# Expert results stored by token through an indirect write, and read back with plain loads, in a one-core decoder layer

## What is computed

```python
def ffn(x, gate_w, gate_b, w1, b1, w2, b2):           # E = 8 experts, K = 2, F = 1024
    gate_probs = softmax(x @ gate_w + gate_b)
    weights, selected = top_k(gate_probs, K)
    weights = weights / sum(weights)
    comb = zeros((n, E)).at[arange(n)[:, None], selected].set(weights)
    h = gelu(einsum('nd,edf->enf', x, w1) + b1[:, None, :])
    expert_out = einsum('enf,efd->end', h, w2) + b2[:, None, :]
    return einsum('ne,end->nd', comb, expert_out)
...
x = layernorm(x + ffn(x, ...))
```

## Time and profile before

| | us |
|---|---|
| median of 3 runs | 587.74 (585.92 to 588.46) |
| time of the profiled execution | 587.59 |
| its span, first to last instruction | 585.5 |
| PE busy (share of the span) | 541.9 (93%) |
| DVE busy | 359.4 (61%) |
| ACT busy | 316.2 (54%) |
| POOL busy | 170.4 (29%) |
| bytes moved by DMA | 58.77 MB, 100 GB/s on average |

### The profile page before, as it was taken

How to read it: one execution, slowest core, us unless ns; L and a number is a source line. 1 busy time by engine, 2 the same in 40 slices (tenths; PEclk the granted TensorE clock), 3 DMA queues, 4 the chain that set the end, 5 groups by cost and what they waited for, 6 DMA issues and landing times. The chain is left out here.

```text
span 585.5 us, 12747 instructions
## 1 busy us (share of the span) xinstructions
PE 541.9 (93%) x3908; PEld 470.8 (80%) x3908; DVE 359.4 (61%) x1136; ACT 316.2 (54%) x862; POOL 170.4 (29%) x280
## 2 busy tenths in 40 slices
PE   5999999999999999999999999989889999999920
PEld 3989899898998989899887666655479999999920
DVE  3365655657556565655567767787585656666645
ACT  4564554645545455454546787756553545545613
POOL 3511312113131221300445758442630000000353
PEclk9999999999999999999999999999799999999975
DMA  7850310405004050182000000020212535444224
GB/s 252 299 198 20 148 69 18 179 18 191 24 28 169 18 197 0 59 346 114 2 2 1 1 3 4 3 74 24 95 46 60 218 137 189 180 181 180 64 81 125
DMA packets 18420, 58.77 MB, mean 100 GB/s; under 512 B 3184, under 2 KB 7536, under 8 KB 13776
## 3 DMA queue, kind: packets, MB, share of 16 engines
q1 hardware_dynamic: 13920, 37.74, 17.9%
q10 hardware_dynamic: 1872, 12.85, 5.8%
q0 software_dynamic: 2592, 7.74, 3.9%
HBM read 35.83 MB, written 22.41 MB: 99 GB/s over the span
## 5 line engine op out<-in xcount | busy, mean ns | idle before, releaser
L1337 ACT ACTIVATE hT<-bank,b 128x128 f32<-128x128 f32 x152 | 53.7, 367 | 60.1 <-PE bank L954 56.5
L954 PE MATMUL bank<-xgT,w 128*128 128x128 f32 x608 | 71.2, 275 | 0.8 <-DVE xgT L1644 0.8
L954 PEld LDWEIGHTS bank<-xgT,w 128*128 128x128 f32 x608 | 69.6, 192 | 1.1 <-issue 1.0
L1089 ACT ACTIVATE Pr<-Sm,nmax 128x128 f32<-128x128 f32 x64 | 25.8, 403 | 70.7 <-DVE nmax L1398 70.6
L616 PE MATMUL bank<-xT_hi,wqk_hi 128*128 128x512 f32 x128 | 56.8, 444 | 7.1 <-DVE wqk_lo L1389 6.4
L1398 DVE CUSTOM_DVE_ANT_0 Sm<-bank,mask 128x128 f32<-128x128 f32 (+1 forms) x128 | 40.7, 355 | 30.2 <-PE bank L660 30.2
L1537 DVE TENSOR_REDUCE xnmax<-bank 128x2 f32<-128x512 f32 x64 | 43.5, 687 | 16.2 <-PE bank L818 15.6
L618 PE MATMUL bank<-xT_hi,wqk_lo 128*128 128x512 f32 x128 | 51.2, 400 | 0.0
L617 PE MATMUL bank<-xT_lo,wqk_hi 128*128 128x512 f32 x128 | 50.8, 397 | 0.0
L1199 ACT ACTIVATE xPT<-bank 128x512 f32<-128x512 f32 x64 | 37.7, 595 | 16.3 <-PE bank L839 16.1
L1420 DVE TENSOR_TENSOR z_lo<-bank,z_hi 128x256 fp32r<-128x256 f32 x64 | 27.1, 423 | 30.7 <-ACT z_hi L1082 30.5
(11 more groups left out here) (245 smaller groups left out, 1491.8 us busy)
## 6 DMA issues: line engine op xcount, KB each, us to landing
w<-in_w ACTq DMA_DIRECT2D x12, 1024.0 KB, 6.2
x_slots<-w SPq DMA_DIRECT2D x8, 1024.0 KB, 5.5
w_raw<-in_w_attn SPq DMA_DIRECT2D x31, 256.0 KB, 3.6
y_slots<-w SPq DMA_DIRECT2D x7, 1024.0 KB, 7.4
w<-in_w SPq DMA_DIRECT2D x4, 1024.0 KB, 7.9
y_slots<-ys POOLq DMA_DIRECT2D x19, 128.0 KB, 2.1
xg<-x_slots SPq DMA_DIRECT2D x18, 128.0 KB, 2.0
acc<-in_x SPq DMA_DIRECT2D x1, 1024.0 KB, 9.0
```

The lines of the kernel that those rows point to most:

```text
L954: last = mm(ps_h[f % 4][:, 0:P], w1[e % 2][:, c, f * P:(f + 1) * P], xgT[:, c, :], start=c == 0, stop=c == DC - 1)
L1337: A(hT[:, f, :], ps_h[f % 4][:, 0:P], ACT.Gelu_apprx_tanh, bias=b1[:, e, f:f + 1])\
```

## The change

- A row of `x_slots` grows from 256 to 258 numbers. The two at its end are the token's row number, 2 + 2\*token, and the lower of its two experts. `acc` gets the two columns in SBUF (`acc_rows`); an iota and one small DVE operation in each `slots(r)` fill them. `x_slots` is filled with zeros in 16 pieces of 128 x 1032 numbers, and `y_slots` with none.
- `y_slots` is replaced by a table `y_rows` of 2050 rows of 256: rows 2 + 2\*token and 3 + 2\*token are a token's results of its lower and its higher expert. Rows 0 and 1 take what unused slots give.
- Per tile, DVE computes `row_i` from the two numbers (`rows_of`), and copies the next tile's two numbers out of `xg` (`token`) right before the copy to `xgT`. POOL stores `ys` by an indirect DMA through `row_i`.
- The wait for the store of the tile before (`y_stored`) leaves `y_add` and now stands in `rows_of`, ahead of the copy to `xgT`. SP loads `xg` after the copy to `xgT` of the tile before (`xgt_ready`) and not after its transposes (`xgt_done`).
- One plain load from POOL brings all of `y_lo`; eight plain loads from SP bring `y_hi`.

The core of the diff:

```diff
+    W = D + 2
+    ZROWS = N // 2
+    ZFILLS = E * CAP // ZROWS
-        acc = sb(ctx, "acc", [P, TT, D])
+        acc_rows = sb(ctx, "acc", [P, TT, W])
+        acc = acc_rows[:, :, 0:D]
...
+        y_pairs = ys_d[2:2 * N + 2, :].rearrange("(t p k) d -> p t k d", p=P, k=2)
...
                 with sp.Fori(lo, hi) as i:
-                    sp.wait_ge(s["xgt_done"], i + 1)
+                    sp.wait_ge(s["xgt_ready"], i)
...
+            sp.wait_ge(s["y_stored"], lo * 16)
+            sp.nop(nofuse=True)
+            for t in range(TT):
+                sp.dma_start(y_hi[:, t, :], y_pairs[:, t, 1, :]).then_inc(s[f"yhi_in{t}"], 16)
...
                         g.indirect_dma_start(xs_d, bass.IndirectOffsetOnAxis(ap=slot_i[:, t, k:k + 1], axis=0),
-                                             acc[:, t, :], None).then_inc(s["xs_written"], 16)
+                                             acc_rows[:, t, :], None).then_inc(s["xs_written"], 16)
...
+            def store_rows():
+                g.indirect_dma_start(ys_d, bass.IndirectOffsetOnAxis(ap=row_i[:, 0:1], axis=0), ys[:, :], None)\
+                    .then_inc(s["y_stored"], 16)
...
-                    for t in range(TT):
-                        g.indirect_dma_start(y_lo[:, t, :], None, ys_d,
-                                             bass.IndirectOffsetOnAxis(ap=slot_i[:, t, 0:1], axis=0))\
-                            .then_inc(s["ylo_in"], 16)
+                    g.dma_start(y_lo[:, :, :], y_pairs[:, :, 0, :]).then_inc(s["ylo_in"], 16)
...
+            def rows_of(e, i, pair):
+                if not (isinstance(i, int) and i == 0):
+                    dve.wait_ge(s["y_stored"], i * 16)
+                v.scalar_tensor_tensor(out=row_i[:, :], in0=pair[:, 1:2], scalar=float(e), in1=pair[:, 0:1],
+                                       op0=ALU.is_lt, op1=ALU.add).then_inc(s["rows_ready"], 1)
+
-            def xgt_evac(count_done):
+            def xgt_evac(count_done, take=True):
                 dve.wait_ge(s["xgt_done"], count_done)
+                if take:
+                    v.tensor_copy(token[:, :], xg[:, D:W]).then_inc(s["token_ready"], 1)
...
             def y_add(e, i):
                 dve.wait_ge(s["y_done"], i + 2)
-                dve.wait_ge(s["y_stored"], i * 16 + 16)
...
                 with dve.Fori(lo, hi) as i:
                     h_splits(i)
+                    dve.wait_ge(s["token_ready"], i + 1)
+                    rows_of(e, i, token[:, :])
+                    dve.wait_ge(s["rows_ready"], i + 1)
                     xgt_evac(i + 3)
                     y_add(e, i)
```

More of the change, by code:

```diff
@@ L107, in build_decoder_layer @@
         w_lh = sb(ctx, "w_lh", [P, TT, 2])
+        token = sb(ctx, "token", [P, 2])
+        row_i = sb(ctx, "row_i", [P, 1], i32)
         tiles_i = sb(ctx, "tiles_i", [P, E], i32)
@@ L179, in build_decoder_layer @@
         hT_lo = sb(s3, "hT_lo", [P, FC, P], f32r)
-        xg = sb(s3, "xg", [P, D])
         xgT = sb(s3, "xgT", [P, DC, P])
-        xg_s = sb(s3, "xg_s", [P, EARLY, D])
+        xg_s = sb(s3, "xg_s", [P, EARLY, W])
         w2_hi1 = sb(s3, "w2_hi1", [P, FC, D], f32r)
+        xg = sb(s3, "xg", [P, W])
         ys = sb(s3, "ys", [P, D])
@@ L287, in _ @@
             half = N // 2
+            zero_rows = w1[0][:, :, :].rearrange("p c f -> p (c f)")[:, 0:ZROWS // P * W]
             for c in range(DC):
@@ L320, in next_parts @@
                 sp.dma_start(w_raw[:, 3, :], w_attn_d[bass.ds(p + 1, 1), :, 3, :]).then_inc(s["wo_in"], 16)
[L321 to L324, removed]
+                for k in range(2):
+                    sp.dma_start(xs_d[bass.ds((2 * p + k) * ZROWS, ZROWS), :].rearrange("(a b) d -> a (b d)", a=P),
+                                 zero_rows).then_inc(s["slots_zeroed"], 16)
                 sp.wait_ge(s["wqk_split"], 2 * p + 4)
@@ L331, in _ @@
             sp.dma_start(w_raw[:, 3, :], w_attn_d[PAIRS - 1, :, 3, :]).then_inc(s["wo_in"], 16)
[L332 to L336, removed]
+            for k in range(2 * (PAIRS - 2), ZFILLS):
+                sp.dma_start(xs_d[k * ZROWS:(k + 1) * ZROWS, :].rearrange("(a b) d -> a (b d)", a=P),
+                             zero_rows).then_inc(s["slots_zeroed"], 16)
+            sp.wait_ge(s["slots_zeroed"], 16 * ZFILLS)
             for e in range(2):
@@ L386, in _ @@
             pool.sem_inc(s["y_evac"], 1)
+            pool.sem_inc(s["token_ready"], 2)
             g.memset(ident[:, :], 0.0).then_inc(s["zeroed"], 1)
@@ L405, in _ @@
                    allow_small_or_imprecise_dtypes=True).then_inc(s["ident_ready"], 1)
+            g.iota(acc_rows[:, :, D], pattern=[[2 * P, TT]], base=2, channel_multiplier=2,
+                   allow_small_or_imprecise_dtypes=True).then_inc(s["ident_ready"], 1)
             g.iota(iota_slot[:, :], pattern=[[CAP, E]], base=0, channel_multiplier=0,
@@ L554, in _ @@
             for e in range(E):
-                skip = pool.value_load(first_i[0:1, e:e + 1], min_val=0, max_val=N // P - 1) if e < EARLY else 0
                 hi = pool.value_load(cum_i[0:1, e:e + 1], min_val=EARLY + 1, max_val=EARLY + 3 * E)
                 if e == E - 1:
-                    pool.wait_ge(s["y_stored"], lo * 16 + 16)
+                    pool.wait_ge(s["y_stored"], lo * 16)
                     pool.nop(nofuse=True)
-                    for t in range(TT):
-                        g.indirect_dma_start(y_lo[:, t, :], None, ys_d,
-                                             bass.IndirectOffsetOnAxis(ap=slot_i[:, t, 0:1], axis=0))\
-                            .then_inc(s["ylo_in"], 16)
+                    g.dma_start(y_lo[:, :, :], y_pairs[:, :, 0, :]).then_inc(s["ylo_in"], 16)
                 with pool.Fori(lo, hi) as i:
                     pool.wait_ge(s["y_evac"], i + 2)
-                    row = nc.s_assert_within((i - lo + skip) * P + e * CAP, e * CAP, (e + 1) * CAP - P,
-                                             skip_runtime_bounds_check_because="an expert has at most CAP tokens")
-                    g.dma_start(ys_d[bass.ds(row, P), :], ys[:, :]).then_inc(s["y_stored"], 16)
+                    pool.nop(nofuse=True)
+                    store_rows()
                 lo = hi
[L571 to L575, removed]
         def o_bank(p, t):
@@ L759, in _ @@
                 v_unit(0, t)
-            pe.wait_ge(s["ident_ready"], 7)
+            pe.wait_ge(s["ident_ready"], 8)
             pairs_loop(pe, attend)
@@ L1774, in _ @@
             gate_select(2)
-            xgt_evac(2)
+            xgt_evac(2, take=False)
             slots(2)
@@ L1784, in _ @@
                 if e == 0:
-                    xgt_evac(e + 3)
+                    rows_of(e, e, xg_s[:, e, D:W])
+                    xgt_evac(e + 3, take=False)
                     y_add(e, e)
@@ L1789, in _ @@
                     slot_weights()
+                    rows_of(e, e, xg_s[:, e, D:W])
+                    xgt_evac(e + 3)
                     y_add(e, e)
-                    xgt_evac(e + 3)
             lo = EARLY
@@ L1881 @@
     slots = g["L0_ffn_w1"].shape[0] * x.shape[0]
-    args.append(nc.dram_tensor("x_slots", (slots, x.shape[1]), mybir.dt.float32, kind="Internal").ap())
-    args.append(nc.dram_tensor("y_slots", (slots, x.shape[1]), mybir.dt.float32, kind="Internal").ap())
+    args.append(nc.dram_tensor("x_slots", (slots, x.shape[1] + 2), mybir.dt.float32, kind="Internal").ap())
+    args.append(nc.dram_tensor("y_rows", (2 * x.shape[0] + 2, x.shape[1]), mybir.dt.float32, kind="Internal").ap())
     out = nc.dram_tensor("out", (P, tiles, x.shape[1]), mybir.dt.float32, kind="ExternalOutput").ap()
```

14 lines of the change are left out of this document (6 added, 8 removed).

## The result

| | before | changed |
|---|---|---|
| median of the timed runs, us | 587.59 (4 runs) | 598.93 (4 runs, 598.19 to 600.85) |
| profiled execution, us | 587.59 | 600.85 |
| its span | 585.5 | 598.6 |

The changed kernel is slower, clear of the noise and by about 2%: 1.0201 times the time before, 95% interval 1.0169 to 1.0234. The forecast was 592.4 us, 584 to 600. So the direction and the range held, but the loss is 11.3 us in the medians where 4.8 were expected. The two profiles lie 13.1 us apart, and the balance goes by them.

The account below looks back on a forecast made before the run. PE was taken as busy nearly all the time until its last matmul at 560.03 us, then a 25.47 us chain follows. 587.59 + 11.6 (waits) - 6.8 (end) = 592.4 us; range 584 to 600.

Parts of the forecast that it names:

- Part 1: Expert tiles: the store wait ahead of the copy to `xgT` makes PE wait six times; PE ends 11.6 us later (0 to 14).
- Parts 2 and 3: Same steps on the other tiles, and routing with its fills and 1032-byte rows: both covered by slack, costing nothing.
- the rival of the slow 1032-byte rows: Last four `x_slots` writes each 1 us slower, PE waiting 2.9 us at 443.57: 595.3 us in all; chance 0.08.
- Part 4: From PE's last matmul to the span's end: 18.6 us against 25.5, 6.9 us less, taken as 6.8.
- the unseen price: POOL's time to issue the single 1 MB load of `y_lo` in 1024 rows: between 0.57 and 8 us.
- The two rivals on an earlier landing: Behind the weights, stores land on their own (580.8 us, chance 0.12) or come about 1 us sooner (585.2 us, chance 0.10).
- The waits cost PE its clock: Rival: PE's clock falls at the waits among the expert tiles, one to six falls, 596 to 613 us; chance 0.10.

Follow-up runs that it names:

- The wait behind the copy: Changed kernel with the wait for the store put back behind the copy to `xgT`, row numbers going through a spare tile first: 582.29 us, ratio 0.9923.
- the wait ahead of it in the kernel before: Kernel before with only the wait for the store moved ahead of the copy to `xgT`, plain stores and gathers kept: 597.82 us, ratio 1.0189.
- The products in the gaps: Changed kernel with four idle products on PE at the end of each tile in the loops: 594.72 us, ratio 1.0153.
- ACT's wait for the store: Changed kernel with ACT issuing the two weight loads only after the store has landed: 613.63 us, ratio 1.0443.

## Why the prediction was wrong in its size

**What held.** *Part 1*: six waits, each behind a pair of weight loads, on DVE `row_i` released by the store. Each was forecast at 1.5 to 2.4 us; five measured 1.60 to 2.02, and one 3.13, where the second MB took 8.8 us to land (7.4 to 8.0 elsewhere) and the store 7.7. The interval from the start of `row_i` to PE's start is 0.91 us (459.48 to 460.39), forecast 0.85. The sum is 12.1 us, forecast 11.6. The wait behind the copy and the wait ahead of it in the kernel before show from both sides that the place of the wait is the cause. *Parts 2 and 3*: no undisturbed tile waits for its store, and routing cost nothing: the opening tile starts within 0.05 us of its old time, so the rival of the slow 1032-byte rows did not occur. *Part 4*: the end is 18.62 us, forecast 18.6. That it is so close is in part luck: the first addition of `y_hi` came 0.14 us later and the chain behind it took 0.13 less. And the issuing of the 1 MB load of `y_lo`, the unseen price, is 0.96 us of POOL. The two rivals on an earlier landing fell: behind the weights the indirect stores landed 6.3 to 7.7 us after their issue, and only where the weights are issued behind the store was that otherwise.

**The step that failed** is the rival "The waits cost PE its clock". It was kept out of the sum, with a chance of 0.10, and the argument against it was that the clock was still 1.00 at 564 us with 4 us of idleness behind it, and that my gaps would be shorter. That row was misread. In it PE does nothing, and the clock fell right behind it, at 565.0 us, so that over the whole of that idle stretch it was 0.60. In the changed kernel it fell 0.3 us after PE had started again behind the gap of 2.02 us: a row from inside an idle stretch doesn't tell what the next products will run at. The row that could have told is the other of the same group. There the clock was 0.58 in a stretch in which PE was busy 3.58 us of 5, and the longest standstill of PE ahead of that fall was only 1.66 us, as short as the gaps of the forecast. The rows, all of the kernel before (PE at this place, then two stretches, with the columns of the earlier trace rows):

```profile
414.93 1.94 PE L855 MATMUL bank<-xPT,Vd 128*32 128x256 f32 x16 [1.66 <-ACT xPT L1199]
415.00:416.00 1.00, 1.00 (x12) 0.59 (x16) 0.73 (x2) 1.00 (x1) 0.95 (x1) 0.50 0.20 70
565.00:566.00 1.00, 0.00 (x0) 0.00 (x0) 1.00 (x4) 0.00 (x0) 0.00 (x0) 0.51 0.36 131
```

The rival's own size was fair: it allowed up to 3.4 us for a fall, and the three took 1.73, 1.73 and 2.82. Three of them are 6.3 us, about the whole of what the forecast missed: 592.4 + 6.3 = 598.7, measured 598.93. The products in the gaps show this: with them the falls are gone, and the same first products take 6.5 us less. The end of the range, 600, held by 1.1 us only, and one fall more would have put the time outside.

**The term that was missing** is small: 1.15 us for the last load of `xg` behind the load of `y_lo`. Part 4 asked what POOL's time for that load would hold back, and not what the load would do to the others in flight. The text named it only for the last stores.

**The sum as measured.** Waits 12.1, clock 6.3, `xg` 1.15, small differences 0.4, the end -6.85: 13.1 us in the profiles, of which the medians show 11.3. The clock also falls once ahead of the experts, at 414 us before and at 389 us after. The time to the opening tile's first product is the same in both, so it is no part of this sum. That it is the same is in part chance: in the version with the wait behind the copy, where this fall is missing, it is 3.2 us shorter.

**What stays open**: what decides, among gaps of 1.78 to 2.04 us, whether the clock falls, and why it fell ahead of the experts after shorter ones (1.66 us before, 1.33 us at 388.59 in the changed kernel). Also what holds a store behind the weights, as said above.

## What to carry to other kernels

A wait in the profile that delays nobody is harmless by its place. Before it is moved on an in-order queue, price it for everything that then stands behind it, less the slack that each of these has; ACT's wait for the store showed the same on another engine. If the moved wait opens gaps in front of PE, add the clock: here five of the eight gaps of 1.78 to 2.04 us and all three of 2.69 to 3.13 us cost 1.7 to 2.8 us on top. Here a short store issued right behind 2 MB of loads landed nearly when they did, so what waits for it has to stand late in its queue, and for every new big load ask who is in flight behind it.

## What the runs showed of the hardware

- PE's granted clock fell to 0.50, its level of 1.2 GHz, behind gaps of 1.78 to 2.04 us (five of eight) between the expert tiles, and stayed there for 3 to 4 us; behind a gap of 3.13 us it was nearly 7 us, which cost 2.82 us. None of the gaps of 1.20 to 1.72 us between these tiles did that. Ahead of the experts it fell at gaps of 1.66 us (before, 414.93) and 1.33 us (changed, 388.59).
- Work that nobody reads took time off a kernel: four idle products a tile cost 10.2 us where PE had no gaps, and took off 4.2 us by the medians where it had six.
- An indirect write of 128 rows of 1 KB took 2.4 to 2.5 us undisturbed, 2.6 to 4.2 with 2 MB issued right behind it by POOL, and 6.3 to 7.7 in the changed kernel with 2 MB issued right ahead of it by ACT.
- A plain load of 1 MB in 1024 rows of 1 KB cost POOL 0.96 us to issue, as much as one indirect write of 128 rows.
